# A two-layer graph kernel: VectorE's rank passes in pieces, and one one-hot per group moved to ScalarE

## The reference

```
h = relu(layernorm(x))
x = x + node_vec1_n2 * segment_sum((h * node_vec1)[src], dst)
h = relu(layernorm(x))
x = x + (1 + eps) * h + segment_sum(relu(h[src] + edge_attr), dst)
```

## Time and profile before

| | us |
|---|---|
| median of three runs | 4991.05 |
| lowest and highest run | 4982.14, 4993.16 |
| the profiled execution's own time | 4992.93 |
| its span | 4991.1 |
| PE, VectorE, ScalarE, GpSimd busy | 3947.7, 3814.8, 2985.4, 3756.2 |

### The profile page before, as it was taken

The page is one execution under the profiler, slowest core; times in us unless marked ns, Lnnn a source line. Parts: engine busy times, 40 slices in busy tenths (PEclk is TensorE's granted clock), DMA queues, the critical chain, the costliest instruction groups (busy, mean ns, idle before and its releaser), DMA issues.

```text
span 4991.1 us, 129116 instructions
## 1 busy us (share of the span) xinstructions
PE 3947.7 (79%) x44428; PEld 2974.3 (60%) x44428; DVE 3814.8 (76%) x11503; ACT 2985.4 (60%) x7899; POOL 3756.2 (75%) x3712
## 2 busy tenths in 40 slices
PE   0688889888888888988888899847777777777775
PEld 0455656666666666666666666636666666666664
DVE  9777878788888888878787888577777777777776
ACT  1456656565656565656566666636666666666664
POOL 6777777777777777777777777747777777777774
PEclk9999999999999999999999999968888888888887
DMA  6222222222222222222222221122222221222221
GB/s 107 53 52 53 53 53 53 53 53 53 53 53 53 53 53 53 53 53 52 53 53 53 53 52 29 31 71 55 56 52 56 55 50 47 52 56 56 56 55 25
DMA packets 437208, 265.05 MB, mean 53 GB/s; under 512 B 330740, under 2 KB 421220, under 8 KB 430120
## 3 DMA queue, kind: packets, MB, share of 16 engines
q1 hardware_dynamic: 318264, 185.91, 16.3%
q0 software_dynamic: 116960, 65.42, 7.5%
q10 hardware_dynamic: 1296, 4.79, 0.3%
HBM read 176.35 MB, written 79.52 MB: 51 GB/s over the span
## 4 chain that ended last, share of the span: by engine, by line
PE 33%; POOL 28%; DVE 20%; issue 14%; ACT 3%; DMA 2%; DVEq 1%; SPq 0%; ACTq 0%; POOLq 0%
PE candidates L1159 21%; POOL stage L697 20%; DVE arena L1638 6%; POOL records L709 6%; PE plain_ps L1171 6%; DVE arena L1619 4%; DVE counts L1386 2%; POOL message L690 2%; PE sorted_agg L1102 1%; PE candidates L1074 1%; ACT arena L820 1%; DVE counts L1394 1%; DVE counts L1389 1%; DMA stage<-in_edge_attr 1%; PE plain_ps L1131 1%
## 5 line engine op out<-in xcount | busy, mean ns | idle before, releaser
L709 POOL DMA_INDIRECT records<-stage,place_i x1875 | 1929.6, 1029 | 593.5 <-issue 570.6
L697 POOL DMA_INDIRECT stage<-table,src_plain x1250 | 1256.7, 1005 | 406.3 <-issue 378.1
L906 ACT ACTIVATE message<-candidates,member_is 128x96 bf16<-128x96 f32 x3600 | 916.6, 352 | 629.8 <-PE candidates L1159 626.8
L1638 DVE TENSOR_SCALAR arena<-window_iota,dst_rel 128x224 bf16<-128x224 f16 (+1 forms) x5000 | 1146.6, 300 | 45.2
L1102 PE MATMUL sorted_agg<-arena 128*96 128x224 bf16 (+1 forms) x5000 | 667.9, 288 | 208.2 <-DVE arena L1638 207.8
L820 ACT ACTIVATE arena<-key_rows 125x640 f16<-125x640 f16 x1000 | 649.1, 707 | 213.4 <-PE key_rows L1056 109.8
L1102 PEld LDWEIGHTS sorted_agg<-arena 128*96 128x96 bf16 x5000 | 550.2, 138 | 238.8 <-DVE arena L1638 237.5
L1619 DVE TENSOR_SCALAR arena<-arena,row_key 125x1280 bf16<-125x1280 f16 x1000 | 566.5, 567 | 136.5 <-ACT arena L820 110.9
L1159 PE MATMUL candidates<-parts,arena 125*128 125x480 bf16 x3072 | 661.8, 366 | 0.0
L690 POOL DMA_INDIRECT message<-table,mid_src x480 | 507.5, 1057 | 146.4 <-issue 143.3
L1056 PE MATMUL key_rows<-ident,record 128*125 128x128 f16 x5000 | 417.4, 233 | 203.8 <-DMA record<-records 114.2
(11 more groups left out here) (222 smaller groups left out, 5053.0 us busy)
## 6 DMA issues: line engine op xcount, KB each, us to landing
record<-records SPq DMA_DIRECT2D x50, 1650.0 KB, 7.5
stage<-in_edge_attr SPq DMA_DIRECT2D x125, 400.0 KB
records<-pad SPq DMA_DIRECT2D x25, 1650.0 KB
records<-stage,place_i POOLq DMA_INDIRECT x1875, 2.2
stage<-table,src_plain POOLq DMA_INDIRECT x1250
message<-table,mid_src POOLq DMA_INDIRECT x480
xs<-in_x SPq DMA_DIRECT2D x8, 390.6 KB
table<-parts ACTq DMA_DIRECT2D x4, 585.9 KB
```

The lines of the kernel that those rows point to most:

```text
L697: pool.indirect_dma_start(message[:, k, j, :] if l == 0 else rows[:, k, j, :], None, table0 if l == 0 else table1, bass.IndirectOffsetOnAx ...
L709: pool.indirect_dma_start(records, bass.IndirectOffsetOnAxis(ap=place_i[:, h, e:e + 1], axis=0), stage[:, h, e, :], None).then_inc(scatter ...
L906: last = nc.scalar.activation(direct_message[n % DB][:, m * WIDE:(m + 1) * WIDE], candidates[n % 2][:, m * WIDE:(m + 1) * WIDE], ACT.Copy, ...
L1638: last = nc.vector.tensor_scalar(dst_onehot(g, t), window_iota[:, 0:WA if tile == 0 else WT], dst_rel[:, h, tile:tile + 1], None, ALU.is_e ...
```

## The change

It has two parts. First, VectorE's long passes of the ranks are cut: each pass of 1250 elements into two halves (`HALVES`), the six scans of 625 into twelve of 300 and 325 (`QUARTERS`), the mask of 3750 into six of 625, and the first fold of 1875 into three of 625. The arithmetic is the same, and so are the semaphores between engines; each piece counts one more step that VectorE waits for itself. Second, in layer one the last (tenth) destination one-hot of the groups 2 to 9 is made by ScalarE in two instructions, `tile_distances` and `tile_onehot`; VectorE makes nine there and stops twice instead of three times, and PE waits for one more semaphore before `products` of these groups. ScalarE's order in group g becomes `copy_keys(g + 3)`, `tile_onehot(g + 1)`, `copy_candidates(g + 2)`, `tile_distances(g + 2)`.

```diff
@@ -409,6 +409,7 @@
         rounds_begun = sem("rounds_begun")
         distances_ready = sem("distances_ready")
         mid_distances_ready = sem("mid_distances_ready")
+        tile_onehot_ready = sem("tile_onehot_ready")
         direct_done = sem("direct_done")
         plain_key_ready = per_layer("plain_key_ready")
         plain_paused = per_layer("plain_paused")
@@ -896,6 +897,19 @@
                     nc.scalar.activation(mid_onehot[:, some, :], mid_onehot[:, some, :], ACT.Relu,
                                          bias=one[:, 0:1], scale=-1.0).then_inc(plain_onehot_ready[0], 1)
 
+                def tile_distances(b, h, g):
+
+                    act.wait_ge(dst_rel_ready[0], b + 1)
+                    act.wait_ge(sorted_done[0], GROUPS * b + g - 1)
+                    tile = g * GROUP + GROUP - 1
+                    nc.scalar.activation(dst_onehot(g, GROUP - 1), window_iota[:, 0:WT], ACT.Abs,
+                                         bias=dst_rel[:, h, tile:tile + 1], scale=-1.0).then_inc(distances_ready, 1)
+
+                def tile_onehot(b, g):
+                    act.wait_ge(distances_ready, (GROUPS - 2) * b + g - 1)
+                    nc.scalar.activation(dst_onehot(g, GROUP - 1), dst_onehot(g, GROUP - 1), ACT.Relu,
+                                         bias=one[:, 0:1], scale=-1.0).then_inc(tile_onehot_ready, 1)
+
                 def copy_wide(b, h, n):
                     side, r = TILE_OF[n]
                     act.wait_ge(wide_picked, DIRECTS * b + n + 1)
@@ -916,10 +930,14 @@
                     def group(g):
                         if g + 3 < GROUPS:
                             copy_keys(b, h, u, g + 3)
+                        if g >= 1 and g + 1 < GROUPS:
+                            tile_onehot(b, g + 1)
                         if g in (7, 8) and not is_last(b):
                             copy_direct_keys(b, g - 7)
                         if g + 2 < GROUPS:
                             copy_candidates(b, h, u, g + 2)
+                        if g >= 0 and g + 2 < GROUPS:
+                            tile_distances(b, h, g + 2)
                     over_main_groups(group)
                     copy_sorted(b, 0)
                     if not is_last(b):
@@ -959,7 +977,7 @@
                         last.then_inc(distances_ready, 1)
 
                 def window_onehots(b, k):
-                    act.wait_ge(distances_ready, 2 * b + k + 1)
+                    act.wait_ge(distances_ready, (GROUPS - 2) * BATCHES + 2 * b + k + 1)
                     nc.scalar.activation(plain_onehot[:, k, :, :], plain_onehot[:, k, :, :], ACT.Relu,
                                          bias=one[:, 0:1], scale=-1.0).then_inc(plain_onehot_ready[1], 1)
 
@@ -1096,6 +1114,8 @@
                     if g == 0:
                         at_least(pe, sorted_copied[l], b - l)
                     pe.wait_ge(dst_onehot_ready[l], nth + 1)
+                    if l == 0 and g >= 2:
+                        pe.wait_ge(tile_onehot_ready, (GROUPS - 2) * b + g - 1)
                     pe.wait_ge(message_ready[l], 2 * nth + 2 if l == 0 else nth + 1)
                     for t in range(GROUP):
                         into = agg if g == 0 and t == 0 else agg[:, UP * (t % 2):UP * (t % 2) + WT]
@@ -1335,7 +1355,10 @@
                     for k in range(CHUNKS):
                         table_parts(l, k)
 
-            RANK1 = 9 + 2 + 5
+            RANK1 = 8 + 2 * SORTED + 4 * SORTED - 1
+
+            HALVES = (slice(0, BUCKETS // 2), slice(BUCKETS // 2, BUCKETS))
+            QUARTERS = [slice(BUCKETS * k // 4 * J, BUCKETS * (k + 1) // 4 * J) for k in range(4)]
 
             def rank_within(b, h, u):
                 nth = [0]
@@ -1355,14 +1378,15 @@
                 step(nc.vector.scalar_tensor_tensor(odd[:], bucket_of[:], -2.0, col_of[:], ALU.mult, ALU.add))
                 step(nc.vector.scalar_tensor_tensor(src_key[:], odd[:], float(P), row_of[:], ALU.mult, ALU.add))
                 for v in range(SORTED):
-                    step(nc.vector.tensor_tensor(
-                        in_bucket[:, v, :].rearrange("p (g j) -> p g j", j=J), bucket_iota[:],
-                        bucket16[:, v * J:(v + 1) * J].unsqueeze(1).to_broadcast([P, BUCKETS, J]), ALU.is_equal))
+                    for half in HALVES:
+                        step(nc.vector.tensor_tensor(
+                            in_bucket[:, v, :].rearrange("p (g j) -> p g j", j=J)[:, half, :], bucket_iota[:, half, :],
+                            bucket16[:, v * J:(v + 1) * J].unsqueeze(1).to_broadcast([P, BUCKETS // 2, J]), ALU.is_equal))
                 for v in range(SORTED):
-                    for some in (slice(0, BUCKETS * J // 2), slice(BUCKETS * J // 2, BUCKETS * J)):
+                    for some in QUARTERS:
                         last = nc.vector.tensor_tensor_scan(counts[:, v, some], not_first[:].rearrange("p g j -> p (g j)")[:, some],
                                                             in_bucket[:, v, some], 0.0, ALU.mult, ALU.add)
-                        if v < SORTED - 1 or some.start == 0:
+                        if v < SORTED - 1 or some.stop < BUCKETS * J:
                             step(last)
                 last.then_inc(scans_ready, 1)
                 assert nth[0] == RANK1
@@ -1371,7 +1395,7 @@
             HALVINGS = []
             while (HALVINGS[-1] if HALVINGS else BUCKETS) > 4:
                 HALVINGS.append(-((HALVINGS[-1] if HALVINGS else BUCKETS) // -2))
-            RANK_SUMS = SORTED + 1 + len(HALVINGS) + 1
+            RANK_SUMS = 2 * SORTED + 2 * SORTED + SORTED + len(HALVINGS) - 1 + 1
             RANK2 = RANK_SUMS + 14
 
             def rank_sums(b):
@@ -1383,15 +1407,20 @@
                     dve.wait_ge(rank2_steps, (b - 1) * RANK2 + nth[0])
                 dve.wait_ge(prefix_copied, b + 1)
                 for v in range(SORTED):
-                    step(nc.vector.tensor_tensor(
-                        counts[:, v, :].rearrange("p (g j) -> p g j", j=J), counts[:, v, :].rearrange("p (g j) -> p g j", j=J),
-                        prefix16[:, v * BUCKETS:(v + 1) * BUCKETS].unsqueeze(2).to_broadcast([P, BUCKETS, J]), ALU.add))
-                step(nc.vector.tensor_tensor(counts[:], counts[:], in_bucket[:], ALU.mult))
+                    for half in HALVES:
+                        step(nc.vector.tensor_tensor(
+                            counts[:, v, :].rearrange("p (g j) -> p g j", j=J)[:, half, :], counts[:, v, :].rearrange("p (g j) -> p g j", j=J)[:, half, :],
+                            prefix16[:, v * BUCKETS:(v + 1) * BUCKETS].unsqueeze(2).to_broadcast([P, BUCKETS, J])[:, half, :], ALU.add))
+                for v in range(SORTED):
+                    for half in HALVES:
+                        some = slice(half.start * J, half.stop * J)
+                        step(nc.vector.tensor_tensor(counts[:, v, some], counts[:, v, some], in_bucket[:, v, some], ALU.mult))
 
                 held = BUCKETS
                 for half in HALVINGS:
-                    others = counts[:, :, half * J:held * J]
-                    step(nc.vector.tensor_tensor(counts[:, :, 0:(held - half) * J], counts[:, :, 0:(held - half) * J], others, ALU.add))
+                    for units in [slice(v, v + 1) for v in range(SORTED)] if held == BUCKETS else [slice(0, SORTED)]:
+                        onto = counts[:, units, 0:(held - half) * J]
+                        step(nc.vector.tensor_tensor(onto, onto, counts[:, units, half * J:held * J], ALU.add))
                     held = half
                 step(nc.vector.reduce_sum(rank[:].rearrange("p (v j) -> p v j", j=J),
                                           counts[:, :, 0:held * J].rearrange("p v (g j) -> p v j g", j=J), AX))
@@ -1633,13 +1662,18 @@
                         dve.wait_ge(dst_rel_ready[l], b + 1)
                     at_least(dve, sorted_done[l], nth - 1)
                     run = 5 if l == 1 else 3
-                    for t in range(GROUP):
+
+                    tiles = GROUP - 1 if l == 0 and g >= 2 else GROUP
+                    paused = nth * ((GROUP - 1) // run)
+                    if l == 0:
+                        paused = (6 + 2 * (GROUPS - 2)) * b + (3 * g if g < 2 else 6 + 2 * (g - 2))
+                    for t in range(tiles):
                         tile = g * GROUP + t
                         last = nc.vector.tensor_scalar(dst_onehot(g, t), window_iota[:, 0:WA if tile == 0 else WT], dst_rel[:, h, tile:tile + 1],
                                                        None, ALU.is_equal)
-                        if t % run == run - 1 and t < GROUP - 1:
+                        if t % run == run - 1 and t < tiles - 1:
                             last.then_inc(dst_paused[l], 1)
-                            dve.wait_ge(dst_paused[l], nth * ((GROUP - 1) // run) + t // run + 1)
+                            dve.wait_ge(dst_paused[l], paused + t // run + 1)
                     last.then_inc(dst_onehot_ready[l], 1)
```

## The result

The median went from 4991.35 us (10 runs) to 5001.62 us (10 runs): a ratio of 1.0023, 95% interval 1.0015 to 1.0032. The change made the kernel slower by about 10 us, 0.2%; the interval leaves 7.5 to 16 us. The profiled execution of the changed kernel took 5002.02 us, with a span of 5000.2.

A forecast was written before the change was run, and what follows sets the result against it. GpSimd and the computing engines were taken to bound layer one almost equally. Terms +1.8, -1.1, -3.6, +7.2 and -2.7 made +1.6 us on the profiled 4992.9: 4994.5, as a median 4992; range 4975 to 5012, no change 0.48.

The forecast's parts named there:

- the second rival: GpSimd loses step with VectorE in the groups: each DMA 1.306 us or above, +1.0 us a batch, 5013 us; chance 0.18.
- GpSimd and the computing chain end together; the computing chain drops out: Layer one's two chains end within 1.1 us; the computing one changes by -10 us and stops being a bound.
- The +2.3 us a batch of that chain: Cut rank passes lengthen the computing chain: 0.3 us uncovered before `prefixes` and 2.0 in `rank_sums`, each batch.
- Durations of the pieces: VectorE's cut rank passes: 625 elements take 495 to 810 ns, scan pieces 785 and 837 ns.
- The ranks are worth nothing to GpSimd: Cutting the rank passes changes GpSimd's DMA waits by near to nothing: 0.15 us a batch gained, -3.6 us over 24.
- the first rival: A shorter pass is a shorter wait: GpSimd's waits in the ranks halve, -1.9 us a batch, 4970 to 4981; chance 0.27.
- The 0.2 us at the start of a pass: Estimate for GpSimd beside the rank passes: a DMA is let in during the first 0.2 us of each VectorE pass.
- Out of step, +0.3 us a batch: In the groups, VectorE's shorter group no longer matches three DMA periods; GpSimd loses a third of 1.0, +7.2 us over 24 batches.
- A group of 3.46 us: VectorE's one-hot group in layer one falls from 3.80 to 3.46 us, 0.34 less by the moved one-hot.
- The start, +1.8: The first scatter waits for VectorE's first ranks, where the extra time of `rank_within` stands uncovered: +1.8 us.
- The last batch, -2.7, and -1.1 for its record: In layer one's last batch the moved one-hots gain 2.7 us in full; its record, taken up on landing, gains 1.1.
- Wrong if PE waits for ScalarE's one-hot: Sign of error: in the groups ScalarE should deliver the moved one-hot in time, so PE should not wait for it.

The follow-up runs named there:

- cut_only: The changed kernel with ScalarE's part out again: cut passes alone, VectorE makes all ten one-hots; 5039.51 us, ratio 1.0094 to the kernel before.
- scans_eight: The changed kernel with the twelve scans of a batch made as eight of 450 and 475 elements; 4985.61 us, ratio 0.9985 to the kernel before.
- Seven scans: The changed kernel with the twelve scans of a batch made as seven of 525 and 550 elements; 4955.83 us, ratio 0.993 to the kernel before.
- the move alone: The kernel before with only the tenth one-hot moved to ScalarE, the ranks' passes whole; 5000.96 us, ratio 1.002.
- moved_vector_as_before: The kernel before with the one-hot moved, but VectorE makes the ninth tile's one-hot twice, with three pauses; 4990.64 us, ratio 1.000.
- ranks_in_step: The changed kernel with seven scans, sums over 24, 42, 42, 42 buckets, mask in two, first fold and bucket passes whole; 4940.95 us, ratio 0.9901.
- scans_whole: The changed kernel with the six scans of 625 put back, all else cut and moved; 4988.22 us, ratio 0.9995 to the kernel before.

## Why the prediction was right, and where not

The forecast was 4992 with no change the likeliest; 5001.62 lies inside the range, and on the edge between "no change" and the second rival. That it came so near is in part luck: at the first gather of layer two this pair of profiles is 21.4 us apart, where the terms of the sum make 1.6. The prediction's own signs of being wrong speak too: GpSimd's batch moved by 0.74 us, to 0.64 above the forecast 126.9, where 0.5 was the limit, and PE does wait for ScalarE's one-hot. Its steps:

- **GpSimd and the computing chain end together; the computing chain drops out.** Right. PE's waits for records came back (176.3 us), the last one in layer one is 5.73 us long, and in cut_only, where the move's relief is missing, the other chain is the bound from the eighth batch on. The +2.3 us a batch of that chain measured 2.77 (129.57 less 126.80).
- **Durations of the pieces.** Right: 496 to 508 ns for the mask and bucket halves, 811 for the sums, 786 and 836 for the scans.
- **The ranks are worth nothing to GpSimd.** Right in the sum, -0.02 against -0.15 us a batch, and the 1.69 us that spoke against the first rival stands in the trace. That a shorter pass is a shorter wait is refuted by eight scans against seven. The 0.2 us at the start of a pass in which a DMA was let in did not hold: scans hold DMAs that begin later than 0.04 us (last section).
- **Out of step, +0.3 us a batch.** This is the term that was mis-sized: the groups lost 0.98 us a batch, and a batch as a whole grew by 0.74 (0.79 with the move alone). I had taken a third, since some batches seemed out of step before; but nearly all were in step, at 0.40 for all their one-hots. The rival's 1.0 was nearer.
- **A group of 3.46 us.** It is 3.30: without a DMA's hold the two source one-hots take 1.13 and not 1.30, which I had read as their own length in the earlier trace rows. The computing chain gained nothing by it, since it waits for records; what a group of 3.46 would have done to GpSimd is not shown.
- **The start, +1.8.** Right, but 3.84 us at the first gather, 3.5 more than before, came on top. That leaves 15.5 of the 20.8 us at the last scatter for the 24 batches, 0.65 each.
- **The last batch, -2.7, and -1.1 for its record.** PE takes up the last record 8.5 us after the end of the last scatter, 1.5 less than before, so the second term is right. From there to the last plain one-hot of layer one it is 1.4 us shorter and not 2.7, and at the first gather of layer two nothing of either is left (21.4 us behind, against 20.8 at the last scatter).
- **"Wrong if PE waits for ScalarE's one-hot."** It does, 26.9 us in 13 waits; moved_vector_as_before, with 39.2 us of them, is as fast as before.

From +21.4 in this pair of profiles to +10 in the medians there is a gap that I can't explain. Layer two differs by 12 us between the two profiles, but why the medians don't show the full loss of layer one stays open.

The Trainium skill ("SBUF — State Buffer", Who interferes with whom) infers that `tensor_tensor` passes don't hold up descriptor writing. Seven scans against eight, 30 us apart with nearly the same scan time, show that scans with two inputs do; for `tensor_tensor` itself, one mask of 3750 elements costs GpSimd 0.90 us a batch and six pieces 0.23 (table above). What the section states of passes in a two-port mode, that the holder keeps the other out for a whole instruction, agrees here for scans: 1.87 us for the DMA that came a moment too late.

## What to carry to other kernels

Where GpSimd issues indirect DMAs without pause and VectorE works beside it, write down the period of a DMA (here 1.262 us) and cut VectorE's long passes so that one pass with its gap is just above it (1.29 to 1.34), not simply shorter: eight scans just below it cost GpSimd as much as six long ones (1.36 and 1.40 us a batch). This is shown for scans; for the sums and the mask only together, by ranks_in_step, and all of it on the two chips where before takes 4991 us. Taking work off an engine that isn't the bound can slow the one that is, if their lists had fallen into step; look for periods that are whole multiples before moving anything. Where two chains end together, relieve the one and cut waits on the other in the same change, and price short instructions from a row of the same size.

## What the hardware showed that I had not expected

- The edge is sharp. In the batches 5 to 24 of scans_eight, 14 DMAs began within 0.04 us after the start of a scan, and took 0.95 to 0.96; the 12 that began 0.04 to 0.08 us after it took 1.85 to 1.87 each (worked out from the trace). 0.04 us of phase decide 0.9 us. The other traces agree: in the changed kernel DMAs that began 0.12 to 0.20 us after the start of a scan all took 1.37 us or more, that is, they were held until its end.
- Where a run of passes meets the first DMA counts too: the same six scans cost GpSimd 1.92 us a batch in before, 1.75 with the move alone and 1.40 in scans_whole. My price of a length, from its spacing alone (0.4 for quarters against halves, measured 0.93), left that out.
- 3.84 us that the trace gives no cause for stand at the first gather of the changed kernel. Of the ten kernels on chips of this speed, the four whose rank passes are all whole have no such wait (0.3 at most), the others one of 2.7 to 3.85. I did not follow it.
- The same kernel took 4991 us on two chips and 8732 and 8734 on two others, with engines idle in waits that the trace gives only as "issue", and GpSimd's DMAs at full pace. What slows those two was not tried.
